# Tile norms to GpSimd, a third score bank and two early up products in the last attention batch

## The chip, the cores and the metric

The kernel runs on one core of a Trainium2 chip. The metric is the device time in microseconds of one execution; lower is better. The kernel before took 509.29 us, the median of three runs (506.84, 510.2 and 509.29).

## The reference

The input is x of shape (16, 256, 128): 16 batches of 256 tokens with 128 features. In float32 the reference computes

```
x = x + layernorm(attention(layernorm(x)))
x = x + layernorm(ffn(layernorm(x)))
```

- attention: 16 heads of width 8, scores = q k^T / sqrt(8), a softmax over 256 keys, and an output projection.
- ffn: a router and experts. logits = x gate^T (32 experts in 8 groups); scores = sigmoid(logits); a bias is added for the choice alone; the best 4 groups by the sum of their two best experts, then the best 6 experts in these; the weights are the chosen scores divided by their sum, times 2.5. Every expert has an up product to 64, relu squared, its weight, and a down product to 128. A shared expert of 256 is added to them. The kernel computes all 32 experts densely, with the square root of each weight multiplied in before the square.

## The kernel before

**Attention.** The loop over batches b = 0 to 15 has 16 head steps s in each batch (in TensorE's program 8 pairs j = 0 to 7 with i = 0, 1). For a head there are scores by query (line 1224), whose row maxima VectorE takes (`row_max`, line 926, 256 of them), and scores by key (line 1230), with the maxima subtracted inside the product, which ScalarE exponentiates (`exp`, line 709, 256 of them). `outputs(b, g, sh)` (line 1282) multiplies the exponentials by the values; its last two groups of a batch, g = 2 and 3, run in the next batch behind j = 0 and j = 1. Scores by query run one and a half batches ahead of those by key (LEAD = 3 half batches, called units u), so VectorE has its last row maximum in the first half of batch 14. GpSimd splits the maxima of a unit in three bf16 parts (`split_max`, lines 515 to 518), TensorE transposes them (`transpose_max`, line 1290), ScalarE copies them (`keep_mT`), and SyncE loads them for the scores by key. The scores by query have three PSUM banks (`pS1`), those by key two (`pS2`): a score waits for the exponential of two scores before.

Per batch there follow transpose_o, transpose_on and project_y (line 1311), with ScalarE and VectorE copies between them, and project_y(b - 1) stands at j = 7 of batch b. For batches up to 11, x four batches ahead is normalised by GpSimd (`norm_x`, line 540), transposed and projected to q and k.

**Feed-forward.** Eight tiles of 512 tokens, each 18 blocks k of the hidden dimension: `up_block` (lines 1347 to 1349, three products in one of four banks `pU`, the first two of which are `pS1[0]` and `pS1[1]`, the others `pS2`), `rect` on VectorE (lines 1065, 1071), `square` on ScalarE (lines 794, 785, 790), and `downs` (line 1363 and lines 1373 to 1375). Beside the blocks of tile i run the routing of tile i + 1 (`route`, eight steps on VectorE), the norms of later tiles, and the residuals.

**Tiles 0 and 1 in the attention.** Their norms run on ScalarE in batches 6 and 9 (`norm_y`) and 8 and 13 (`norm_x1`), each four activations (line 658) at s in NORM_S = (1, 4, 7, 8); the small chains of statistics to scale and shift run on GpSimd (`chain_y`, `chain_x1`, lines 344 to 357). Tile 0 is routed between row maxima by ROUTE_FIRST: steps 0 and 1 in batch 13 at s = 12 and 14, steps 2, 3 and 4 in batch 14 at s = 8, 10 and 12, steps 5, 6 and 7 in batch 15 at s = 1, 3 and 5. Its square roots are taken on VectorE without a table (`first_root`, lines 1043 to 1051, with `root_t` in the tile `comb`), in batch 14 at s = 12; step 5 waits for them. Between steps 6 and 7, `root_of_sum` (line 555) is a power on GpSimd. Step 7 ends with `c_done`; TensorE's transpose_c(0) (line 1333) waits for it at j = 4 of batch 15, ahead of outputs(15, 0, 0) and transpose_o(14); ScalarE's keep_cT(0) comes at s = 9; SyncE writes the result and broadcasts it in groups to `c_ring` (line 466).

high_x(0) (ScalarE, s = 4 of batch 15) and low_x(0) (VectorE, line 1057, s = 6) split the tile's transposed x in two parts that the up products need. After batch 15 TensorE's order is outputs(15, 2), a wait for all exponentials, up_block(0, 0), outputs(15, 3), up_block(0, 1), transpose_x1(1) (line 1319), up_block(0, 2), logits(1) (line 1327).

Each engine runs its program in order. `Link` marks an instruction whose successor waits for its semaphore.

Of the kernel before, what the change touches and what calls it, by code (L numbers as in the profile page):

```python
# [28 lines left out]
I32 = mybir.dt.int32  # L29
# [4 lines left out]
P = 128  # L34
# [17 lines left out]
S1_RING, S2_RING = 3, 2  # L52
SCALE = float(DK) ** -0.5
# [29 lines left out]
ROUTE_FIRST = {(NB - 3, 12): 0, (NB - 3, 14): 1, (NB - 2, 8): 2, (NB - 2, 10): 3, (NB - 2, 12): 4, (NB - 1, 1): 5,  # L83
               (NB - 1, 3): 6, (NB - 1, 5): 7}
FIRST_ROOT = (NB - 2, 12)
PREP = (5, 8)
NORM_S = (1, 4, 7, 8)
# [26 lines left out]
def block_kernel(nc, x, wqk, wvo, route_in, up, shup, down, shdown,  # L114
                 ident_b, out):
    with ExitStack() as ctx:
# [78 lines left out]
        root_t = comb  # L195
# [28 lines left out]
        pF = [pS1[2][:, :], pY[:, :]]  # L224
        pN = pO[:, :, :].rearrange("p a b -> p (a b)")
# [93 lines left out]
        block = ctx.enter_context(nc.Block())  # L319

# [170 lines left out]
        def _(pool):  # L491
# [60 lines left out]

            def root_of_sum(i):
                pool.wait_ge(wsum_done, i + 1)
                nc.gpsimd.tensor_tensor(w_root[:, :], w_sum[:, :], power[:, 0:C4], ALU.pow).then_inc(wroot_done, 1)

# [45 lines left out]
            for u in range(NU):  # L602
                split_max(u)
                if u == 27:
                    split_down()
                if u == 0:
                    part3(nc.gpsimd, pool.wait_ge, 2)
                    chain_x(1, FIRST, NT)
                if u % 2 == 0 and u >= 2:
                    if u // 2 + 3 < NB:  # L610
                        norm_x(u // 2 + 3)
                    if u // 2 + 2 < NB:
                        part2(u // 2 + 2)
                        part3(nc.gpsimd, pool.wait_ge, u // 2 + 2)

                    if CUT_BATCH + 2 <= u // 2 < CUT_BATCH + 2 + NCUT:
                        low_up(u // 2 - CUT_BATCH - 2)

                for i in range(2):
                    if u == 2 * PREP[i] + 3:  # L620
                        chain_y(i)
                    if u == 2 * PREP[i] + 5:
                        residual1(i)
                    if u == 2 * PREP[i] + 7:
                        chain_x1(i)
            root_of_sum(0)
# [29 lines left out]
        def _(act):  # L656
# [46 lines left out]
            def exp(b, s):  # L703
                j, hh = s // 2, KEY_HEADS[s % 2]
                n = 2 * NBLK * b + s
                if b >= 1:
                    act.wait_ge(pv_done, 4 * (b - 1) + j // 2 + 1)
                act.wait_ge(s2_done, n + 1)
                nc.scalar.activation(probs[j][:, hh], pS2[n % S2_RING][:, :, :], ACT.Exp,  # L709
                                     scale=SCALE).then_inc(exp_done, 1)  # L710

# [116 lines left out]
            for b in range(NB):  # L828
                proj = b + AHEAD < NB
                last = b == NB - 1  # L830
                for s in range(H):
# [9 lines left out]
                    if s == 4 and last:  # L841
# [16 lines left out]
                    if b - 1 in PREP and s in NORM_S:  # L858
                        norm_y(PREP.index(b - 1), NORM_S.index(s))
                    if b == PREP[0] + 3 and s in NORM_S:  # L860
                        norm_x1(0, NORM_S.index(s))
                    if b == NB - 3 and s in NORM_S:
                        norm_x1(1, NORM_S.index(s))
# [36 lines left out]
        def _(dve):  # L900
# [138 lines left out]
            def first_root(link):  # L1039

                every = [t[:, :, :] for t in (score, root_v, root_h, root_t, root)]
                value, v, half, t, r = every
                link(nc.vector.tensor_scalar(v, value, 1e-36, None, ALU.max))
                nc.vector.tensor_scalar(half, v, -0.5, None, ALU.mult)
                link(nc.vector.tensor_scalar(r.bitcast(I32), v.bitcast(I32), -0.5, float(RSQRT_MAGIC),
                                             ALU.mult, ALU.add))
                for _ in range(3):
                    link(nc.vector.tensor_tensor(t, r, r, ALU.mult))
                    link(nc.vector.tensor_tensor(t, t, half, ALU.mult))
                    link(nc.vector.scalar_tensor_tensor(out=r, in0=t, scalar=1.5, in1=r, op0=ALU.add, op1=ALU.mult))  # L1050
                nc.vector.tensor_tensor(r, r, value, ALU.mult).then_inc(root_done, 1)

# [69 lines left out]
            for b in range(NB):  # L1122
                last = b == NB - 1
                for s in range(H):
# [11 lines left out]
                    if last and s == 6:  # L1136
# [5 lines left out]
                    if (b, s) == FIRST_ROOT:  # L1142
                        first_root(Link(dve, root_link, 0))
# [54 lines left out]
        def _(pe):  # L1198
# [28 lines left out]
            def key_scores(u, k, i, sh):  # L1227
                slot, n = u % RING, 2 * (UB * u + k) + i
                rows = slice(HALF * KEY_HEADS[i], HALF * KEY_HEADS[i] + DIFF_ROWS)
                return mm(pS2[n % S2_RING][:, sh], kp[slot][rows, k, P * sh:P * (sh + 1)], qp[slot][rows, k, :],  # L1230
# [9 lines left out]
            def key_scores_free(u, k, i):  # L1240
# [3 lines left out]
                if n >= S2_RING:  # L1244
                    pe.wait_ge(exp_done, n - S2_RING + 1)
# [176 lines left out]
            for b in range(NB):  # L1422
                proj = b + AHEAD < NB
                last = b == NB - 1
                for j in range(NBLK):
                    uq, uk, k = 2 * b + LEAD + j // UB, 2 * b + j // UB, j % UB
                    for i in range(2):
                        if uq < NU:
                            scores_by_both(uq, uk, k, i)
                        else:  # L1430
                            scores_by_key(uk, k, i)
                    if j in (0, 1) and b >= 1:
# [55 lines left out]
            for sh in range(TH):  # L1488
                outputs(NB - 1, 2, sh)

            pe.wait_ge(max_done, H * NB)
            pe.wait_ge(exp_done, TH * NBLK * NB)
            for i in range(NTILE):
                for k in range(FBLK):
                    n = FBLK * i + k
                    up_block(i, k)
                    downs(n)
                    if i == 0 and k == 0:
                        for sh in range(TH):
                            outputs(NB - 1, 3, sh)  # L1500
# [66 lines left out]
```

## Time and profile before

| | |
|---|---|
| median of the runs shown | 509.29 us |
| the profiled execution | 507.4 us, with a span of 505.6 us |
| TensorE busy | 461.5 us (91%) |
| VectorE busy | 392.6 us (78%) |
| ScalarE busy | 360.2 us (71%) |
| GpSimd busy | 232.2 us (46%) |
| mean granted TensorE clock | 0.989 of full speed |

The span is the time from the first to the last instruction of one profiled execution; 1.8 us of its time lie around it. "PE" is TensorE's matrix products, "PEld" its weight loads, DVE VectorE, ACT ScalarE, POOL GpSimd. Matrix products are pipelined, so a busy PE need not be at its peak: the spacing of starts tells more than the durations. A row of the timeline has start, duration, engine, line, operation and tiles, and in brackets the idle time before it and what ended it. A row of the windows has its stretch (here from one project_y to the next, called a batch), its length, then for PE, PEld, DVE, ACT and POOL the busy time with the number of instructions, the granted TensorE clock as a share of full speed, the DMA share and GB/s.

### The profile page before, as it was taken

To read this page: it belongs to the slowest core of one execution; us is meant where nothing else is said; L and a number is where in the kernel's file an instruction comes from. 1 tells how busy PE (TensorE), PEld (TensorE's weight loads), DVE (VectorE), ACT (ScalarE), POOL (GpSimd) and SP (SyncE) were. 2 spreads that over 40 slices of the span, in tenths; PEclk is the share of its full clock that TensorE was granted. 3 is DMA by queue.
4 is the path that set the end of the run, shared out by engine and by line. 5 is a ranking of instruction groups with operands and counts; after the bars stand their busy time and mean duration, and the time that the engine had idled before them with its cause. 6 is when DMAs were issued, how large, how long until landed. Compare 5 with 4: busy or idle time off the path is not lost.

```text
span 505.6 us, 10660 instructions
## 1 busy us (share of the span) xinstructions
PE 461.5 (91%) x3328; PEld 265.6 (53%) x3328; DVE 392.6 (78%) x1013; ACT 360.2 (71%) x723; POOL 232.2 (46%) x551
## 2 busy tenths in 40 slices
PE   2467999999999999998899899999999999999994
PEld 2222444444444444543346566666666666666662
DVE  3688888889899889989726969595977869596453
ACT  3314888888989888887847586878788777867552
POOL 7055333336555635320113646748384664716351
PEclk9999999999999999999979999999999999999998
DMA  7543344444444444420024263456253544535331
GB/s 205 161 135 120 116 122 124 145 141 145 136 123 149 141 144 138 135 68 3 3 102 160 82 206 132 168 147 211 101 186 117 152 167 177 183 107 209 128 103 41
DMA packets 49047, 67.45 MB, mean 133 GB/s; under 512 B 3808, under 2 KB 35808, under 8 KB 48992
## 3 DMA queue, kind: packets, MB, share of 16 engines
q1 hardware_dynamic: 48992, 66.78, 41.2%
q8 instruction: 27, 0.44, 0.3%
q14 instruction: 28, 0.23, 0.1%
HBM read 51.17 MB, written 15.20 MB: 131 GB/s over the span
## 4 chain that ended last, share of the span: by engine, by line
PE 75%; DVE 10%; issue 8%; ACT 5%; POOL 1%; DMA 0%; POOLq 0%; DVEq 0%; ACTq 0%
PE pO L1282 10%; PE pS L1224 9%; PE pY L1363 8%; PE pS L1363 8%; PE pS L1347 6%; PE pS L1348 6%; PE pS L1349 6%; DVE mneg L926 6%; PE pS L1230 3%; PE pX L1209 2%; PE pY L1299 2%; ACT probs L709 2%; PE pX L1212 2%; PE pY L1311 2%; DVE q_rest L906 1%
## 5 line engine op out<-in xcount | busy, mean ns | idle before, releaser
L926 DVE TENSOR_REDUCE mneg<-pS 128x2 f32<-128x512 f32 x256 | 162.7, 685 | 16.5 <-PE pS L1224 15.8
L709 ACT ACTIVATE probs<-pS 128x512 f32<-128x512 f32 x256 | 142.5, 596 | 25.8 <-PE pS L1230 24.1
L1224 PE MATMUL pS<-qk 48*128 48x256 bf16 x512 | 87.9, 288 | 17.7 <-DVE mneg L926 9.2
L794 ACT ACTIVATE h_ring<-r 128x512 f32<-128x512 f32 x104 | 64.3, 624 | 36.9 <-DVE r L1071 26.4
L1230 PE MATMUL pS<-qk 51*128 51x256 bf16 x512 | 88.6, 280 | 2.2 <-ACT probs L709 2.2
L1347 PE MATMUL pS<-qk,up_hi 128*128 128x512 f32 x144 | 88.5, 614 | 0.0
L1282 PE MATMUL pO<-probs,vv 128*32 128x256 f32 x1024 | 73.6, 394 | 0.0
L1224 PEld LDWEIGHTS pS<-qk 48*128 48x128 bf16 x512 | 33.5, 96 | 69.4 <-DVE mneg L926 46.6
L1071 DVE SCALAR_TENSOR_TENSOR r<-pS,probs 128x512 f32<-128x512 f32 x64 | 43.6, 689 | 27.4 <-PE pS L1349 26.5
L1349 PE MATMUL pS<-qk,up_lo 128*128 128x512 f32 x144 | 56.9, 395 | 0.0
L1348 PE MATMUL pS<-qk,up_hi 128*128 128x512 f32 x144 | 56.9, 395 | 0.0
L1363 PE MATMUL pS<-h_ring,down_sb 128*128 128x512 f32 x104 | 53.2, 593 | 1.9 <-ACT h_ring L794 1.9
L1363 PE MATMUL pY<-h_ring,down_sb 128*128 128x512 f32 x104 | 52.8, 592 | 0.0
L1071 DVE SCALAR_TENSOR_TENSOR r<-pS,c_ring 128x512 f32<-128x512 f32 x64 | 43.6, 687 | 11.6 <-PE pS L1349 8.6
L515 POOL TENSOR_TENSOR m_parts<-mneg,m_zero 128x16 bf16<-128x16 f32 x32 | 7.0, 220 | 93.5 <-DVE mneg L926 93.5
L598 POOL TENSOR_TENSOR h_lo<-probs,h_hi 128x512 fp32r<-128x512 f32 x26 | 33.4, 1288 | 24.7 <-ACT h_hi L785 17.2
L785 ACT ACTIVATE h_hi<-r 128x512 fp32r<-128x512 f32 x40 | 25.3, 632 | 25.3 <-DVE r L1071 25.3
L1282 PEld LDWEIGHTS pO<-probs,vv 128*32 128x32 f32 x1024 | 25.3, 110 | 26.0 <-issue 17.6
L1347 PEld LDWEIGHTS pS<-qk,up_hi 128*128 128x128 f32 x144 | 27.2, 189 | 20.6 <-issue 15.5
L1348 PEld LDWEIGHTS pS<-qk,up_hi 128*128 128x128 f32 x144 | 27.3, 190 | 18.9 <-issue 17.3
L1230 PEld LDWEIGHTS pS<-qk 51*128 51x128 bf16 x512 | 32.3, 95 | 8.8 <-ACT probs L709 5.4
L1349 PEld LDWEIGHTS pS<-qk,up_lo 128*128 128x128 f32 x144 | 27.1, 188 | 6.3
(188 smaller groups left out, 812.4 us busy)
## 6 DMA issues: line engine op xcount, KB each, us to landing
c_ring<-c_scratch SPq DMA_DIRECT2D x32, 512.0 KB, 3.9
probs<-c_scratch SPq DMA_DIRECT2D x32, 512.0 KB, 3.8
qk<-qk_scratch SPq DMA_DIRECT2D x64, 192.0 KB
qk_scratch<-q_parts SPq DMA_DIRECT2D x16, 192.0 KB, 2.3
qk_scratch<-k_parts SPq DMA_DIRECT2D x16, 192.0 KB, 2.3
qk_scratch<-q_parts SPq DMA_DIRECT2D x16, 128.0 KB, 2.2
qk_scratch<-k_parts SPq DMA_DIRECT2D x16, 128.0 KB, 2.1
out_x<-probs SPq DMA_DIRECT2D x7, 256.0 KB, 4.6
```

The costliest lines, as they stand in the source:

```text
L598: nc.gpsimd.tensor_tensor(h_lo[at % LO_RING], h_whole[at % HI_RING], h_hi[at % HI_RING].bitcast(F32), ALU.subtract).then_inc(lo_done, 1)
L709: nc.scalar.activation(probs[j][:, hh], pS2[n % S2_RING][:, :, :], ACT.Exp, scale=SCALE).then_inc(exp_done, 1)
L794: nc.scalar.activation(h_ring[:, (n - at) % HRING], r_sb[n % URING][:, :], ACT.Square).then_inc(sq_done, 1)
L926: nc.vector.tensor_reduce(mneg[u % 2][:, :, hh, k], pS1[n % S1_RING][:, :].rearrange("p (a s) -> p a s", a=TH), AX.X, ALU.max, negate=True ...
L1071: nc.vector.scalar_tensor_tensor(out=r_sb[n % URING][:, :], in0=pU[n % URING], scalar=0.0, in1=c_ring[group % CRING][:, at], op0=ALU.max, ...
L1224: return mm(pS1[n % S1_RING][:, T * th:T * (th + 1)], qp[slot][rows, k, P * th:P * (th + 1)], kp[slot][rows, k, :], start=True, stop=True)
L1230: return mm(pS2[n % S2_RING][:, sh], kp[slot][rows, k, P * sh:P * (sh + 1)], qp[slot][rows, k, :], start=True, stop=True)
L1282: ins = mm(pO[VC * h:VC * (h + 1), half], weights, probs[2 * g + h // 2][:, h % 2, sh, :], start=second == 0 and sh == 0, stop=second == 1 ...
L1347: mm(bank, up_hi[:, block], x_hi[i % 2], start=True, stop=False)
L1348: mm(bank, up_hi[:, block], x_lo[i % 2], start=False, stop=False)
L1349: mm(bank, up_lo[:, block], x_hi[i % 2], start=False, stop=True).then_inc(up_done, 1)
L1363: mm(pF[i % 2], down_sb[:, block], h_ring[:, (n - splits_to(n)) % HRING], start=k == 0, stop=False).then_inc(down_done, 1)
```

## The change

1. Scores by key of batch 15 rotate over three banks (`pLate`: both of `pS2` and `pS1[2]`, which the scores by query no longer use).
2. up_block(0, 0) and up_block(0, 1) are issued in batch 15, behind the scores of j = 2 and j = 3. After the batch, outputs(15, 2) and outputs(15, 3) come directly one after the other, then the blocks from k = 2 on.
3. The sixteen activations of norm_y(0), norm_x1(0), norm_y(1) and norm_x1(1) become sixteen tensor_scalar on GpSimd (`norm_early`), at units 13, 17, 19 and 27. split_down moves from unit 27 to 29.
4. ROUTE_FIRST: steps 0 to 5 in batch 14 at s = 8, 10, 11, 12, 13, 15, steps 6 and 7 in batch 15 at s = 0 and 1.
5. first_root runs on GpSimd, after its last split_max and ahead of root_of_sum(0); a scalar_tensor_tensor of each Newton step becomes a tensor_scalar and a tensor_tensor: 16 instructions, 14 of them linked. `root_t` moves to `yn`.
6. high_x(0) moves from batch 15 to batch 14 (s = 4), low_x(0) from batch 15, s = 6, to batch 14, s = 13.

```diff
-ROUTE_FIRST = {(NB - 3, 12): 0, (NB - 3, 14): 1, (NB - 2, 8): 2, (NB - 2, 10): 3, (NB - 2, 12): 4, (NB - 1, 1): 5,
-               (NB - 1, 3): 6, (NB - 1, 5): 7}
-FIRST_ROOT = (NB - 2, 12)
+ROUTE_FIRST = {(NB - 2, 8): 0, (NB - 2, 10): 1, (NB - 2, 11): 2, (NB - 2, 12): 3, (NB - 2, 13): 4, (NB - 2, 15): 5,
+               (NB - 1, 0): 6, (NB - 1, 1): 7}
...
+        pLate = [pS2[0], pS2[1], pS1[2][:, :].rearrange("p (a t) -> p a t", a=TH)]
...
+            def first_root(link):
+                every = [t[:, :, :] for t in (score, root_v, root_h, root_t, root)]
+                value, v, half, t, r = every
+                pool.wait_ge(score_done, 1)
+                link(nc.gpsimd.tensor_scalar(v, value, 1e-36, None, ALU.max))
+                nc.gpsimd.tensor_scalar(half, v, -0.5, None, ALU.mult)
+                link(nc.gpsimd.tensor_scalar(r.bitcast(I32), v.bitcast(I32), -0.5, float(RSQRT_MAGIC),
+                                             ALU.mult, ALU.add))
+                for _ in range(3):
+                    link(nc.gpsimd.tensor_tensor(t, r, r, ALU.mult))
+                    link(nc.gpsimd.tensor_tensor(t, t, half, ALU.mult))
+                    link(nc.gpsimd.tensor_scalar(t, t, 1.5, None, ALU.add))
+                    link(nc.gpsimd.tensor_tensor(r, r, t, ALU.mult))
+                nc.gpsimd.tensor_tensor(r, r, value, ALU.mult).then_inc(root_done, 1)
...
+            def norm_early(tile, out_, rs, nm, i, ready, used, done):
+                pool.wait_ge(ready, i + 1)
+                if i >= 1:
+                    pool.wait_ge(used, i)
+                for c in range(C4):
+                    ins = nc.gpsimd.tensor_scalar(out_[:, c], tile[:, C4 * i + c], rs[:, c:c + 1], nm[:, c:c + 1],
+                                                  ALU.mult, ALU.add)
+                ins.then_inc(done, 1)
...
                     if u == 2 * PREP[i] + 3:
                         chain_y(i)
+                        norm_early(ybig, yn, rs2, nm2, i, ln2_done, x1_done, yn_done)
...
+                    if u == (2 * PREP[0] + 7, 2 * NB - 5)[i]:
+                        norm_early(xbig, xn2, rs3, nm3, i, ln3_done, x2T_done, xn2_done)
+            first_root(Link(pool, root_link, 0))
             root_of_sum(0)
...
-                if n >= S2_RING:
-                    pe.wait_ge(exp_done, n - S2_RING + 1)
+                if n == N_LATE + S2_LATE - 1:
+                    pe.wait_ge(max_done, H * NB)
+                elif n >= S2_RING:
+                    pe.wait_ge(exp_done, n + 1 - (S2_RING if n < N_LATE + S2_LATE else S2_LATE))
...
+                    if last and j in (2, 3):
+                        pe.wait_ge(max_done, H * NB)
+                        up_block(0, j - 2)
...
-            pe.wait_ge(max_done, H * NB)
-            pe.wait_ge(exp_done, TH * NBLK * NB)
+            for sh in range(TH):
+                outputs(NB - 1, 3, sh)
+
             for i in range(NTILE):
                 for k in range(FBLK):
                     n = FBLK * i + k
-                    up_block(i, k)
+                    if n >= 2:
+                        up_block(i, k)
```

## Rows read from the trace of the kernel before

**Rows 1.** The page: span, busy engines, the chain's shares.

```profile
span 505.6 us, 10660 instructions
PE 461.5 (91%) x3328; PEld 265.6 (53%) x3328; DVE 392.6 (78%) x1013; ACT 360.2 (71%) x723; POOL 232.2 (46%) x551
PE 75%; DVE 10%; issue 8%; ACT 5%; POOL 1%; DMA 0%; POOLq 0%; DVEq 0%; ACTq 0%
```

**Rows 2.** Windows, batches 6 to 9: length, PE, PEld, DVE, ACT, POOL busy, PEclk.

```profile
121.83:135.83 14.00, 13.12 (x155) 6.52 (x153) 12.51 (x24) 12.68 (x29) 9.07 (x22) 1.00 0.45 131
135.83:149.28 13.45, 13.07 (x155) 6.47 (x153) 12.52 (x26) 11.55 (x25) 6.69 (x20) 1.00 0.44 136
149.28:163.28 14.00, 13.11 (x155) 6.53 (x153) 13.07 (x28) 12.53 (x29) 8.75 (x27) 1.00 0.46 138
163.28:177.45 14.17, 13.19 (x155) 6.57 (x153) 12.37 (x23) 12.41 (x28) 8.38 (x21) 1.00 0.45 139
```

**Rows 3.** Instructions of lines 658 and 540: min/median/max ns.

```profile
L658 ACT ACTIVATE yn<-ybig,nm,rs x8: 483/496/502, 125.2 to 172.8; 128x128 f32<-128x128 f32 x8
L540 POOL TENSOR_SCALAR xn<-xbig,rs,nm x24: 447/448/453, 45.4 to 194.7; 128x128 f32<-128x128 f32 x24
```

**Rows 4.** Timeline of batch 6: last split_max instruction, norm_x, and TensorE's transpose_max.

```profile
125.03 0.22 POOL L518 TENSOR_TENSOR m_parts<-m_rest,m_parts 128x16 bf16<-128x16 f32 x1
125.24 0.88 POOL L540 TENSOR_SCALAR xn<-xbig,rs,nm 128x128 f32<-128x128 f32 x2
127.96 0.28 PE L1290 MATMUL pX<-idb,m_parts 128*24 128x128 bf16 x2
```

**Rows 5.** Waits of batch 14, then windows: batch 14, batch 15.

```profile
PE pS L1224 <- DVE mneg L926: 1.1, 3, 0.5
231.10:244.45 13.35, 11.69 (x133) 5.18 (x131) 11.77 (x42) 9.99 (x20) 1.77 (x8) 1.00 0.01 3
244.45:259.67 15.22, 13.29 (x109) 4.87 (x107) 7.36 (x32) 10.41 (x22) 1.02 (x1) 0.78 0.19 75
```

**Rows 6.** Windows of batch 15: the slow exponentials, then the half clock.

```profile
248.80:251.80 3.00, 1.44 (x8) 0.35 (x7) 1.76 (x12) 2.95 (x7) 1.02 (x1) 1.00 0.00 0
252.00:258.50 6.50, 6.50 (x47) 2.16 (x45) 1.42 (x4) 2.76 (x7) 0.00 (x0) 0.50 0.34 133
```

**Rows 7.** Timeline, batch 15: exponentials, transpose_c, two up blocks, transpose_x1.

```profile
244.61 2.30 ACT L709 ACTIVATE probs<-pS 128x512 f32<-128x512 f32 x4
252.34 0.47 PE L1333 MATMUL pX<-wqk_sb,root_c 128*128 128x128 f32 x1
261.31 0.50 PE L1347 MATMUL pS<-qk,up_hi 128*128 128x512 f32 x1
263.22 0.50 PE L1347 MATMUL pS<-qk,up_hi 128*128 128x512 f32 x1
264.03 0.60 PE L1319 MATMUL pX<-wqk_sb,xn 128*128 128x128 f32 x4
```

**Rows 8.** Last row maxima, window to step 7, a root instruction, step 7.

```profile
238.45 1.28 DVE L926 TENSOR_REDUCE mneg<-pS 128x2 f32<-128x512 f32 x2
239.72:251.66 11.94, 10.31 (x108) 4.19 (x106) 8.90 (x51) 9.97 (x20) 1.91 (x5) 1.00 0.02 4
244.10 0.29 DVE L1048 TENSOR_TENSOR comb<-root 128x128 f32<-128x128 f32 x1
251.66 0.39 DVE L1034 SCALAR_TENSOR_TENSOR root_c<-root_c,w_root 128x128 f32<-128x128 f32 x1 [1.14 <-POOL w_root L555]
```

**Rows 9.** GpSimd's tensor_tensor on 256 elements, by its line (min/median/max ns).

```profile
L335 POOL TENSOR_TENSOR k_parts<-k_rest,k_parts x14: 667/669/672, 32.3 to 210.7; 128x256 bf16<-128x256 f32 x14
```

**Rows 10.** A VectorE instruction beside a GpSimd one, and its spread.

```profile
280.65 1.29 POOL L598 TENSOR_TENSOR h_lo<-probs,h_hi 128x512 fp32r<-128x512 f32 x1 [1.62 <-ACT h_hi L785]
280.74 1.35 DVE L1020 SCALAR_TENSOR_TENSOR comb<-e_left,score 128x128 f32<-128x128 f32 x1
L1020 DVE SCALAR_TENSOR_TENSOR comb<-e_left,score x8: 293/746/1351, 249.4 to 452.2; 128x128 f32<-128x128 f32 x8
```

More of the change, by code:

```diff
@@ L52 @@
 S1_RING, S2_RING = 3, 2
+S2_LATE, N_LATE = 3, H * (NB - 1)
 SCALE = float(DK) ** -0.5
@@ L81 @@
 NORM_X1_AT = ((12, 13, 14, 15), (11, 12, 13, 14))
-ROUTE_FIRST = {(NB - 3, 12): 0, (NB - 3, 14): 1, (NB - 2, 8): 2, (NB - 2, 10): 3, (NB - 2, 12): 4, (NB - 1, 1): 5,
-               (NB - 1, 3): 6, (NB - 1, 5): 7}
-FIRST_ROOT = (NB - 2, 12)
+ROUTE_FIRST = {(NB - 2, 8): 0, (NB - 2, 10): 1, (NB - 2, 11): 2, (NB - 2, 12): 3, (NB - 2, 13): 4, (NB - 2, 15): 5,
+               (NB - 1, 0): 6, (NB - 1, 1): 7}
 PREP = (5, 8)
-NORM_S = (1, 4, 7, 8)
 LAG = 3
@@ L194, in block_kernel @@
         root_v, root_h = (sb(n, [P, C4, E]) for n in ("root_v", "root_h"))
-        root_t = comb
+        root_t = yn[:, 0, :].rearrange("p (c e) -> p c e", c=C4)
         cT = sb("cT", [P, P])
@@ L319, in block_kernel, with s2_bank @@
         block = ctx.enter_context(nc.Block())
+        def s2_bank(n):
+            return pS2[n % S2_RING] if n < N_LATE else pLate[(n - N_LATE) % S2_LATE]
         def x1_bank(i):
@@ L603, in _ @@
                 split_max(u)
-                if u == 27:
+                if u == 29:
                     split_down()
@@ L708, in exp @@
                 act.wait_ge(s2_done, n + 1)
-                nc.scalar.activation(probs[j][:, hh], pS2[n % S2_RING][:, :, :], ACT.Exp,
+                nc.scalar.activation(probs[j][:, hh], s2_bank(n)[:, :, :], ACT.Exp,
                                      scale=SCALE).then_inc(exp_done, 1)
@@ L840, in _ @@
                         keep_cT(0)
-                    if s == 4 and last:
+                    if s == 4 and b == NB - 2:
                         high_x(0)
@@ L856, in _ @@
                         part1_q(b + AHEAD)
[L858 to L863, printed above, removed]
             for i in range(NTILE):
@@ L1037, in route @@
                     assert link.n == RT_LINKS, link.n
[L1039 to L1051, printed above, removed]
             def low_x(i):
@@ L1135, in _ @@
                         keep_y(b - 1)
-                    if last and s == 6:
+                    if b == NB - 2 and s == 13:
                         low_x(0)
@@ L1141, in _ @@
                         stats_x1(PREP.index(b - 2))
-                    if (b, s) == FIRST_ROOT:
-                        first_root(Link(dve, root_link, 0))
                     if (b, s) in ROUTE_FIRST:
@@ L1229, in key_scores @@
                 rows = slice(HALF * KEY_HEADS[i], HALF * KEY_HEADS[i] + DIFF_ROWS)
-                return mm(pS2[n % S2_RING][:, sh], kp[slot][rows, k, P * sh:P * (sh + 1)], qp[slot][rows, k, :],
+                return mm(s2_bank(n)[:, sh], kp[slot][rows, k, P * sh:P * (sh + 1)], qp[slot][rows, k, :],
                           start=True, stop=True)
@@ L1495, in _ @@
                     n = FBLK * i + k
-                    up_block(i, k)
+                    if n >= 2:
+                        up_block(i, k)
                     downs(n)
-                    if i == 0 and k == 0:
-                        for sh in range(TH):
-                            outputs(NB - 1, 3, sh)
                     if i == 0:
```

## The prediction, written before the changed kernel ran

> **What bounds the kernel now.** I read the page first: TensorE is busy for 91% of the span, and the chain of waits lies on it for 75% [rows 1]. A moved piece of another engine's work therefore pays only where TensorE stands still for it, and I looked for those places.
>
> First the windows from one project_y to the next, one per batch. Batch 7 takes 13.45 us. Batches 6, 8 and 9, the ones with four norms on ScalarE, take 14.00, 14.00 and 14.17, with 13.1 us of TensorE work as in batch 7 and 0.9 to 1.1 us more of ScalarE [rows 2]. The norms cost batch time although no engine is full.
>
> Then the waits of batch 14: scores stand 1.1 us for row maxima [rows 5], which come late because routing steps 0 and 1 sit between them.
>
> Then batch 15, 15.22 us at a mean clock of 0.78 [rows 5]. Between 248.8 and 251.8 ScalarE is busy for 2.95 of 3 us and TensorE for 1.44; behind that the granted clock is 0.50, the level of 1.2 GHz instead of 2.4, for 6.5 us in which TensorE is busy without a gap [rows 6]. The clock fell after TensorE had been half idle.
>
> **Norms on GpSimd.** Sixteen activations of 0.49 us leave ScalarE; sixteen tensor_scalar of 0.448 us come to GpSimd, 1.8 us per group [rows 3]. Back come 0.55 + 0.55 + 0.72 = **1.8 us** in batches 6, 8 and 9 [rows 2]. Queued behind a group on GpSimd are split_max and norm_x. In batch 6 the split ends at 125.25, norm_x about 0.9 us later, and TensorE takes the maxima at 127.96 [rows 4]; 1.8 us later is 127.05, still 0.9 us ahead. part2 and part3 follow, whose scratch writes SyncE sends before it loads the next maxima; those are used half a batch later. I cost this at nothing; without the cover each of three batches would lose up to 1.8 us. split_down's move has no one waiting. For batch 13 no like batch exists; I take 0.4 us of the 0.6 us that the others show (bounds 0 and 0.7).
>
> **Batches 13 and 14.** Routing steps 0 and 1 leave the row maxima: 1.1 us of waits back [rows 5]. high_x(0) enters ScalarE's queue ahead of the exponential of s = 5, 0.6 us, and TensorE is two exponentials behind it: I charge it in full. Net 0.5 us, **0.9 us** with batch 13's norm.
>
> **Batch 15, until c_done.** (Times as in this trace, without the gains so far.) From 244.45 TensorE has before transpose_c the projection (0.65), five pairs of scores (2.0), two output groups (2.0) and now two up blocks: 0.8 us each by their starts (263.22 to 264.03) [rows 7]. That is 6.3 us. ScalarE, freed of high_x, must have done nine exponentials (0.575 each) [rows 7] and one copy, which ends near 250.3, and the last scores follow. TensorE reaches transpose_c at 251.0 rather than 252.34, with both up blocks behind it. They fill the hole that precedes the half clock.
>
> But c_done must be there. VectorE ends its row maxima at 239.7 [rows 8]. From there to step 7 it is busy for 8.9 of 11.9 us today, of which the thirteen root instructions, 0.29 us and less with 0.04 between them, are 3.8 [rows 8]. In the new order, by the durations of the same instructions: step 0 takes 1.2 us, norm_o(13) lasts until 242.0 (it waits for TensorE), steps 1 and 2 1.6 us, step 3 1.5, low_x 0.7, step 4 and keep_y 0.7, the first part of step 5 1.5. VectorE asks for the roots at 248.0. GpSimd starts at about 241.0, behind its last split_max, four instructions of 0.3 us by their starts. Its tensor_tensor on 128 elements is not in the trace; it lies between 0.22 us for 16 elements [rows 4] and 0.67 for 256 [rows 9], and its tensor_scalar is 0.448 [rows 3]. I take 0.40 for both, near the middle, and 0.08 for each link: 16 x 0.48 = 7.7, roots at 248.7 (bounds 0.30 and 0.67 each: 247 and 253). Selection, step 6, the power with its hand-over (1.14) and step 7 (0.39) [rows 8] take 2.4 us: c_done at about 251.0. There would be no wait.
>
> The trace speaks against that [rows 10]. Routing's comb instruction takes 0.293 us alone and 1.351 beside a GpSimd subtraction: it started 0.1 us into it and ended 0.15 us after it. A VectorE instruction that reads two SBUF tiles stood until GpSimd's ended. Now eleven such instructions of steps 1, 2 and 4, low_x and the selection meet a row of root instructions. The eight of steps 1 and 2 go in five linked groups; one GpSimd period per group is some 0.4 us more, **2.0 us** in all with low_x (bounds 0 and 11 x 0.4 = 4.4). Then VectorE asks for the roots at about 250, c_done is at 253.0, and TensorE waits 2.0 us at transpose_c.
>
> The Trainium skill (SBUF — State Buffer, "Who interferes with whom") calls this a lock of a shared port pair: a VectorE instruction with two SBUF inputs and a GpSimd one that reads SBUF exclude each other, and the later one fully blocks. The row above agrees with it; leaving it out would make the sum 2.0 us better.
>
> The same skill (GPSIMD Engine Reference, 3.1) gives tensor_tensor on 2048 elements 1.96 times VectorE's time. An estimate from that page and VectorE's 0.29 [rows 8] would be 0.57 each, roots at 251.4, and 1.4 us less gain. No run here shows it.
>
> **Behind c_done.** Before, 252.34 to 264.03 took 11.7 us [rows 7]. Off that go the two up blocks (0.9 + 0.8) and half of the 6.5 us at half clock, 3.25, if the clock holds: 6.75 us remain. From 253.0 that is 259.75, against 264.03: **4.3 us**. Rectified blocks 0 and 1 come during the last outputs, as VectorE waits there; c_ring, loaded some 6 us after c_done, arrives by 259, ahead of block 2. The third bank lets scores run one exponential ahead and is in the 251.0.
>
> Sum: 1.8 + 0.9 + 4.3 = **7.0 us**. The profiled execution took 507.4 us (span 505.6), 1.9 under the median; against it the changed kernel would take 500.4, against the median of 509.3, by which it will be judged, 502.3.
>
> **Rivals.**
> 1. No lock worth its name: c_done at 251.0, gain 9.0, 500.3 us. For it: VectorE's instructions may slip into the gaps of linked ones. Against: the stretched instruction [rows 10]. Chance 0.15.
> 2. The clock still falls. The wait at transpose_c is an idle stretch just where it fell before [rows 6]; then 3.25 us do not come back: gain 3.75, 505.5 us. Against: the up blocks keep TensorE full until it. Chance 0.22.
> 3. The norms give nothing, since another wait takes their place (split_max behind GpSimd's norms, or VectorE, busy 12.5 of 13.5 us [rows 2]): 2.2 us less, 504.5 us. Against: the batch without norms is short. Chance 0.08.
> 4. Slower: roots on GpSimd far too late, with TensorE and ScalarE standing at transpose_c. Lock waits already put VectorE's demand at 250; the gain is gone when roots come 7.0 us later, at 257 (1.0 us an instruction), or with the half clock at 253.8 (0.8 each, over the 0.67 of 256 elements [rows 9]). At 1.2 us each with the half clock: 260, loss of 6 us, 515 us. Chance 0.07.
> 5. The ordering changes but nothing moves, because TensorE's work alone fills batches 14 and 15: its busy 11.69 of 13.35 us [rows 5] speaks against it. Chance 0.03, 507.5 us.
>
> The forecast has 0.45. **Chances.** 1% is 5.1 us, about what a measurement of this kernel can tell. The forecast (gain 5.5 to 8.2) and rival 1 are faster; of rivals 2 and 3 a sixth; faster 0.64. The rest of 2, 3 and 5 are same, 0.29; rival 4 is slower, 0.07. The **range** goes from 499.3 (no lock and a 1 us better batch 13) to 507.3 (half clock, and batch 6 to 9 giving half).
>
> **What would show it.** Batches 6, 8, 9 at 13.45 us; no wait of transpose_max for GpSimd; the granted clock 1.00 through batch 15; two up blocks near 249 and 250; root instructions at 0.40 us with VectorE's routing stretched beside them; a wait of 2 us at transpose_c; transpose_x1(1) some 7 us earlier. The prediction fails if c_done comes before TensorE asks or after 255, if the clock falls, or if batches 6 and 9 keep 14 us.

## The result, and the profile after

The changed kernel takes 502.1 us (median of 4, 501.69 to 502.27) against 509.75 for the kernel before on the same chip (506.84 to 510.43): ratio 0.987 with a 95% interval of [0.983, 0.991], faster by 1.3%. A second series gave 502.0 against 509.1, ratio 0.986 [0.983, 0.988]. The forecast was 502.3. "Half clock" below is a granted TensorE clock of 0.50. The profiled execution took 502.27 us, before it was 507.4.

The page of the changed kernel (span; busy time of each engine; shares of the chain of waits), beside [rows 1]:

```profile
span 500.4 us, 10661 instructions
PE 460.5 (92%) x3328; PEld 266.2 (53%) x3328; DVE 390.0 (78%) x1000; ACT 354.2 (71%) x707; POOL 248.1 (50%) x583
PE 75%; DVE 10%; issue 7%; POOL 4%; ACT 3%; DMA 0%; POOLq 0%; DVEq 0%; ACTq 0%
```

TensorE's busy time is 1.0 us lower, ScalarE's 6.0, and GpSimd's 15.9 higher: a page like this shows where work went, not where time came from. That is in the windows. Of the changed kernel, columns as in [rows 2]; first batches 6 to 9, then batch 14 and batch 15, then two stretches at half clock, one in batch 14 and one in tile 0:

```profile
122.68:136.04 13.36, 12.98 (x155) 6.55 (x153) 12.32 (x24) 11.38 (x25) 10.77 (x26) 1.00 0.44 131
136.04:149.49 13.45, 13.07 (x155) 6.47 (x153) 12.51 (x26) 11.55 (x25) 6.72 (x20) 1.00 0.49 140
149.49:162.94 13.45, 13.07 (x155) 6.47 (x153) 12.76 (x27) 11.31 (x25) 10.34 (x30) 1.00 0.47 140
162.94:176.31 13.37, 12.99 (x155) 6.55 (x153) 12.32 (x24) 10.92 (x24) 10.21 (x26) 1.00 0.47 142
229.24:243.11 13.87, 12.80 (x133) 5.71 (x131) 11.42 (x36) 10.20 (x21) 6.08 (x18) 0.88 0.01 3
243.11:254.63 11.52, 10.99 (x114) 4.92 (x113) 5.69 (x27) 9.57 (x21) 4.83 (x8) 1.00 0.05 16
237.20:240.60 3.40, 3.40 (x25) 1.40 (x28) 1.84 (x5) 1.43 (x4) 2.84 (x8) 0.50 0.01 2
278.20:281.60 3.40, 3.40 (x9) 1.87 (x8) 1.99 (x4) 1.82 (x4) 3.00 (x8) 0.50 0.30 120
```

Against [rows 2] and [rows 5], one profiled execution against the other, step by step:

| stretch | before | after | gain | predicted |
|---|---|---|---|---|
| batches 6, 8, 9 | 14.00, 14.00, 14.17 | 13.36, 13.45, 13.37 | 2.0 | 1.8 |
| batches 13 and 14 | 13.47 + 13.35 | 12.76 + 13.87 | 0.2 | 0.9 |
| batch 15's start to transpose_x1(1) | 19.58 | 14.03 | 5.55 | 4.3 |
| tile 0, transpose_x1(1) to transpose_x1(2) | 28.35 | 29.87 | -1.5 | 0 |
| from there to the end, and start-up | | | -1.0 | 0 |

The sum is 5.2 us, the difference of the spans, and not 7.0. The start-up is 0.85 us of the last row (batch 3 begins at 82.50 instead of 81.65, ahead of everything that was changed). Over the thirteen traces of altered kernels that start lies between 82.50 and 83.94, so a difference of one us between two single traces can be start-up alone.

TensorE's timeline of the changed kernel (start, duration, instruction, idle time ahead of it and what ended it). Beside [rows 7]: the last two waits of batch 14 ahead of the half clock, the up blocks, transpose_c, transpose_x1(1), and the hole of tile 0:

```profile
235.68 0.27 PE L1235 MATMUL pS<-qk 48*128 48x256 bf16 x1 [0.58 <-ACT probs L742]
236.40 0.84 PE L1241 MATMUL pS<-qk 51*128 51x256 bf16 x4 [0.32 <-ACT probs L742]
247.24 0.50 PE L1360 MATMUL pS<-qk,up_hi 128*128 128x512 f32 x1
248.51 0.50 PE L1360 MATMUL pS<-qk,up_hi 128*128 128x512 f32 x1
250.02 0.30 PE L1346 MATMUL pX<-wqk_sb,root_c 128*128 128x128 f32 x1 [0.22 <-DVE root_c L1061]
257.14 0.66 PE L1332 MATMUL pX<-wqk_sb,xn 128*128 128x128 f32 x4
276.87 1.12 PE L1376 MATMUL pS<-h_ring,down_sb 128*128 128x512 f32 x2 [2.10 <-ACT h_ring L827]
```

The up blocks sit where the change puts them, batch 15 keeps the granted clock at 1.00, and TensorE waits for c_done only 0.22 us. But the half clock has not gone away. It now comes at 237.2 in batch 14 and at 278.2 in tile 0, the first time behind waits of 0.58 and 0.32 us, the second behind one of 2.10 us.

### The profile page after: what moved, and what is told of

It is laid out like the page before. It is cut to its first block, busy times and chain, and to the rows that moved or that the text cites. A ratio compares the mean times of both kernels' runs of the same rounds, so it can differ in the third digit from the quotient of the medians.

```text
span 500.4 us, 10661 instructions
## 1 busy us (share of the span) xinstructions
PE 460.5 (92%) x3328; PEld 266.2 (53%) x3328; DVE 390.0 (78%) x1000; ACT 354.2 (71%) x707; POOL 248.1 (50%) x583
## 4 chain that ended last, share of the span: by engine, by line
PE 75%; DVE 10%; issue 7%; POOL 4%; ACT 3%; DMA 0%; POOLq 0%; DVEq 0%; ACTq 0%
PE pO L1295 10%; PE pS L1235 9%; PE pY L1376 8%; PE pS L1376 8%; PE pS L1360 6%; PE pS L1362 6%; PE pS L1361 6%; DVE mneg L953 5%; PE pS L1241 3%; PE pX L1220 2%; PE pY L1312 2%; PE pY L1324 2%; PE pX L1223 2%; DVE q_rest L933 1%; PE pX L1215 1%
## 5 line engine op out<-in xcount | busy, mean ns | idle before, releaser
L1241 PE MATMUL pS<-qk 51*128 51x256 bf16 x512 | 86.6, 280 | 0.5 <-ACT probs L742 0.3
L1084 DVE SCALAR_TENSOR_TENSOR r<-pS,probs 128x512 f32<-128x512 f32 x64 | 43.6, 689 | 29.1 <-PE pS L1362 28.1
```

The lines of the kernel that those rows point to most:

```text
L1084: nc.vector.scalar_tensor_tensor(out=r_sb[n % URING][:, :], in0=pU[n % URING], scalar=0.0, in1=c_ring[group % CRING][:, at], op0=ALU.max, ...
L1241: return mm(s2_bank(n)[:, sh], kp[slot][rows, k, P * sh:P * (sh + 1)], qp[slot][rows, k, :], start=True, stop=True)
```

## The experiments

Each was run against the kernel before on its chip. The kernel before had medians of 509.0 to 509.4 there. Ratios are to it, with 95% intervals. "Through to x1" is the time in the profiled run from the start of batch 14 to transpose_x1(1): 32.93 us before, 27.90 changed.

**The changed kernel once more.**

> The changed kernel itself again, for the spread of its runs beside those of the kernel before. Theory (a fall of the clock in batch 14 costs it little, since c_done is late anyway, and one in tile 0 costs 1.5 us, whereas a fall in the kernel before costs 1.5 to 4 us): its runs lie within 501 to 503, those of the kernel before within 505.5 to 510.5; the fastest of each are 4 to 5 us apart, the medians 7. Rival (the difference is the same whatever the clock does): the fastest runs are 7 us apart as well.

502.01 us (500.20 to 503.35), 0.986 [0.983, 0.988]. The medians are 7.1 us apart, the fastest executions of this series 6.05: between theory and rival. Over all series the fastest are 505.54 and 500.20, 5.3 apart. Its profiled run shows batch 14 without a half clock: 12.51 us, batch 15 12.68, through to x1 27.70. The same code had one half clock less, and the difference in this stretch was 0.2 us: with it TensorE arrives late, without it TensorE waits. Window of its batch 14, and its transpose_c:

```profile
230.55:243.06 12.51, 11.44 (x133) 5.25 (x131) 10.96 (x31) 10.27 (x21) 4.96 (x15) 1.00 0.01 3
251.12 0.30 PE L1346 MATMUL pX<-wqk_sb,root_c 128*128 128x128 f32 x1 [1.23 <-DVE root_c L1061]
```

**Norms back on ScalarE**, all else changed.

```
-        norm_early(...)                      # both calls, GpSimd
+        if b - 1 in PREP and s in NORM_S: norm_y(...)     # ScalarE, as before
+        if b == PREP[0] + 3 and s in NORM_S: norm_x1(0, ...)
```

> The changed kernel with the sixteen norms of tiles 0 and 1 back on ScalarE. Theory (the norms cost TensorE time only in their own batches): batches 6, 8 and 9 take 14.0, 14.0 and 14.2 us again, 2.0 us more in all, and batch 13 up to 0.5 us more; batch 15 unchanged; 2.0 to 2.5 us slower than the changed kernel, about 504.4. Rival (in the new schedule the norms are hidden, and batches 6 to 9 got faster by something else): those batches stay at 13.4 us and the time at 502.

503.42 us (502.19 to 505.71), 0.990 [0.987, 0.994]: 1.4 us slower by the medians, where 2.0 to 2.5 were expected. Batches 6, 8, 9 are back at 14.01, 14.00, 14.18, batch 13 at 13.47: 2.0 + 0.7 us in the trace. Batch 14 took 15.18 us here, with 6.6 us at half clock (its window), and lost 1.2 us more, through to x1 29.11:

```profile
241.00:247.60 6.60, 6.60 (x47) 2.15 (x48) 4.59 (x19) 3.20 (x6) 5.54 (x14) 0.50 0.01 2
```

**Norms alone**: the kernel before, with norm_early and split_down as in the changed one.

```
+        norm_early(...)      # GpSimd, units 13, 17, 19, 27; ScalarE's sixteen activations gone
-        if u == 27:
+        if u == 29:          # split_down
```

> The kernel before with only the sixteen norms (and split_down) moved to GpSimd. Theory: batches 6, 8 and 9 at 13.4 us, 2.0 us less together, batch 13 shorter by 0.3 to 0.7 us, batches 14, 15 and tile 0 as before; 506.5 to 507. Rival (half clocks and later waits take it back): within 1 us of the kernel before.

506.54 us (505.13 to 507.92), 0.997 [0.995, 0.999]. Batches 6, 8, 9 and 13 are as short as in the changed kernel. Its batch 15, which has the old order, had no half clock in the profiled run and took 12.56 us instead of 15.22; through to x1 was 30.32. This is the order of before without its half clock, and so tells the two parts of the 5.55 us apart. Its hole is the one of [rows 6] to the hundredth, TensorE busy for 1.44 of 3.00 us (last window), and no half clock followed: the hole by itself does not make the fall.

```profile
123.33:136.70 13.37, 12.99 (x155) 6.55 (x153) 12.32 (x24) 11.38 (x25) 10.73 (x26) 1.00 0.42 129
243.30:255.86 12.56, 10.69 (x109) 4.40 (x107) 7.36 (x32) 10.34 (x22) 1.02 (x1) 1.00 0.04 13
247.65:250.65 3.00, 1.44 (x8) 0.35 (x7) 1.76 (x12) 2.91 (x6) 1.02 (x1) 1.00 0.00 0
```

**Routing alone**: the changed kernel with norms on ScalarE, two banks and late up blocks (the edits of three other runs together).

> The kernel before with the new routing steps, the roots on GpSimd, high_x(0) and low_x(0) in batch 14, and outputs(15, 3) ahead of the up blocks; norms on ScalarE, two banks, up blocks behind the outputs. Theory (routing out of the row maxima gives 1 us in batches 13 and 14, c_done comes 1 us earlier, the hole of batch 15 and a half clock stay): 506.5 to 508.5. Rival (the roots' chain is the gain, the up blocks only follow it): 504.5 or less.

509.46 us (506.37 to 509.85), 1.000 [0.998, 1.002], outside what either theory or rival expected. Through to x1 was 29.90 in the profiled run, at 506.37 the fastest of the twelve; it had 3.4 us of half clock in batch 14 and none in batch 15, where the two up blocks were missing. By itself the new routing order shows no gain in the medians. TensorE stood for exponentials in batch 15 instead:

```profile
251.40 0.88 PE L1245 MATMUL pS<-qk 51*128 51x256 bf16 x4 [0.75 <-ACT probs L740]
```

**Up blocks back behind the outputs.**

```
-                    if last and j in (2, 3):
-                        pe.wait_ge(max_done, H * NB)
-                        up_block(0, j - 2)
...
-                    if n >= 2:
-                        up_block(i, k)
+                    up_block(i, k)
```

> The changed kernel with up_block(0, 0) and (0, 1) issued behind outputs(15, 3) again. Theory (they fill a hole that otherwise also lets the clock fall): batch 15 shows 1.5 us of idle TensorE before transpose_c and a granted clock of 0.50 behind it, transpose_x1(1) comes 3 to 5 us later, time 505 to 507. Rival (the early c_done and the freed ScalarE keep TensorE fed): the clock stays at 1.00 in batch 15 and the blocks cost just their 1.7 us, time 503.8.

506.23 us (504.67 to 507.25), 0.995 [0.993, 0.997]: 4 us of the gain are gone. The half clock was there three times in the profiled run, in batch 14, from 252.8 to 256 in batch 15 and from 283.3 in tile 0, and through to x1 took 30.78. In batch 15 TensorE waits 1.2 us in three places ahead of transpose_c, the longest of them:

```profile
249.48 0.39 PE L1241 MATMUL pS<-qk 51*128 51x256 bf16 x2 [0.59 <-ACT probs L742]
```

**Two banks for the last scores.**

```
-            return pS2[n % S2_RING] if n < N_LATE else pLate[(n - N_LATE) % S2_LATE]
+            return pS2[n % S2_RING]
```

> The changed kernel with two banks for the scores by key of batch 15. Theory (TensorE's own work sets batch 15, as it waits only 0.2 us for c_done and 0.2 us for a copy): within 0.3 us of the changed kernel. Rival (the third bank carries the gain of batch 15): waits of scores for exponentials of 0.3 to 0.6 us each come back between 247 and 250, batch 15 longer by 1 to 2 us, perhaps with a half clock behind them.

502.03 us, 0.988 [0.985, 0.991]; batches 14 and 15 take 12.51 + 12.87 us (12.51 + 12.68 with three banks), through to x1 27.88. The third bank is worth 0.2 us in these two traces and nothing that the medians (502.0 both) can tell.

**Roots on VectorE**, at the place where GpSimd's are wanted.

```
+                    if (b, s) == (NB - 2, 14):
+                        first_root(Link(dve, root_link, 0))    # the function of before
```

> The changed kernel with the thirteen root instructions on VectorE again, at s = 14 of batch 14, ahead of routing step 5; routing, up blocks, banks and norms as changed. Theory (transpose_c waits for c_done, which the roots bound): VectorE has 3.8 us more in its chain, less the 0.4 to 1.1 us that it waited for GpSimd and less 0.5 us that its two-input instructions lost beside GpSimd; c_done 2 to 3 us later against the last row maximum, TensorE waits 2 to 4 us at transpose_c, time 503.5 to 505. Rival (the shared access to SBUF made the move worthless): c_done not later than in the changed kernel, time 502 or below.

506.31 us (503.28 to 508.26), 0.994 [0.992, 0.997]: 4.3 us slower than with GpSimd's roots, and beyond the 503.5 to 505 expected. c_done came 14.7 us after the last row maximum (13.1 and 12.9 with GpSimd's roots), batch 15 takes 15.95 us and a half clock follows the wait (254.5 to 258); the sum of the theory had no term for that. It also gives the price of VectorE's routing instructions when GpSimd is silent. TensorE's transpose_c and VectorE's masked:

```profile
253.11 0.30 PE L1345 MATMUL pX<-wqk_sb,root_c 128*128 128x128 f32 x1 [3.09 <-DVE root_c L1044]
```

```profile
244.39 0.28 DVE L1023 TENSOR_TENSOR masked<-choice,picked_g 128x128 f32<-128x128 f32 x1
```

**Six Newton steps instead of three** (twelve more linked GpSimd instructions, the computation otherwise the same).

```
-                for _ in range(3):
+                for _ in range(6):
```

> The changed kernel with six Newton steps instead of three on GpSimd: twelve more linked instructions of 0.58 us, 7.0 us. A price for a late c_done. Theory (TensorE and ScalarE stand at transpose_c until it comes): roots 7.0 us later, VectorE's wait for them from 0.4 to about 7.5 us, wait at transpose_c about 7 us, a half clock behind it (1.5 to 3.5 us more): 508.5 to 512, the changed kernel's whole gain and more. Rival (the wait is absorbed, since ScalarE catches up on exponentials and later work is moved in): under 4 us slower, below 506.

512.24 us (509.2 to 513.38), 1.005 [1.003, 1.007]: the rival of late roots, made real. VectorE waits 7.64 us, TensorE 7.72, and the clock is at half for ten us, from within that wait (254.5 to 264.7):

```profile
258.29 0.45 PE L1346 MATMUL pX<-wqk_sb,root_c 128*128 128x128 f32 x1 [7.72 <-DVE root_c L1061]
255.70 0.39 DVE L1052 SCALAR_TENSOR_TENSOR root_c<-e_left,root 128x128 f32<-128x128 f32 x1 [7.64 <-POOL root L571]
```

**high_x(0) behind the exponentials that TensorE waits for.**

```
-                    if s == 4 and b == NB - 2:
+                    if s == 9 and b == NB - 2:
                         high_x(0)
```

> The changed kernel with high_x(0) behind the exponential of s = 9 of batch 14 instead of s = 4. Theory (high_x ahead of the exponential of s = 5 makes the 0.6 and 0.3 us waits of TensorE near 235, and the half clock from 237.2 to 240.6 follows from them): those waits shrink below 0.4 us in all, the clock stays at 1.00 in batch 14, batch 14 takes 12.0 to 12.5 us instead of 13.9, time 500.5. Rival (the hole comes from row maxima and the end of the scores by query, whatever ScalarE does): the clock falls there again, gain under 0.5 us.

502.58 us, 0.988 [0.985, 0.991], not the 500.5 expected. The two waits become one of 0.41 us and batch 14 has no half clock, but neither had it in four of the seven traces with the old waits, so this does not show that high_x made the fall. Against the second profiled run of the changed kernel, batch 14 falls from 12.51 to 12.04 us, batch 15 rises from 12.68 to 12.90: c_done is late by then, and the wait at transpose_c grows from 1.23 to 1.46 us. A half clock in tile 0 (277.3 to 280.8) as in the changed kernel.

**The same, with the three head instructions of the roots on VectorE**, behind step 0 (tensor_scalar, 0.22 to 0.23 us each on VectorE; 0.56, 0.54 and 0.30 on GpSimd).

```
+                    if (b, s) == (NB - 2, 8):
+                        root_head(Link(dve, root_link, 0))
...
-                link(nc.gpsimd.tensor_scalar(v, value, 1e-36, None, ALU.max))   # and the two behind it
+                pool.wait_ge(root_link, 2)
```

> high_x(0) at s = 9 of batch 14 as in the fourth experiment, and the three first root instructions on VectorE, where it waits for transpose_o(13), with GpSimd starting at the first Newton step. Theory (behind an unslowed batch 14 the roots set c_done and TensorE waited 1.5 us for it): roots 1.7 us earlier, VectorE's wait of 1.1 us for them gone, the wait at transpose_c 0.6 us or less; about 1 us faster than the fourth experiment, 501 to 501.5. Rival (the lost time comes back at the next wait, ScalarE's exponentials): no change against it.

502.23 us (500.61 to 502.74), 0.987 [0.984, 0.990]: 0.35 us under the fourth experiment's edit alone, where 1 was expected. VectorE no longer waits for roots, the wait at transpose_c is 0.94 us, through to x1 26.94. The profiled run is the 500.61 one, and has no half clock between the first batch and the last tile.

**Tile 2's norm and residual taken out of tile 0**: stats_y(2) in batch 15, then norm and residual on GpSimd before the down products begin. The same work leaves tile 0, where the norm ran on ScalarE, so the edit changes place and engine together.

```
+                    if last and s == 10:
+                        stats_y(2)
...
             chain_y(2)
+            norm_early(ybig, yn, rs2, nm2, 2, ln2_done, x1_done, yn_done)
+            residual1(2)
```

> The changed kernel with tile 2's first norm and residual out of tile 0: stats_y(2) on VectorE at s = 10 of batch 15, chain_y(2), the four normalising instructions and residual1(2) on GpSimd before tile 0. Theory (the 2.1 us hole of TensorE near 275, behind which the clock fell, comes from VectorE standing 1.4 us for x1 of tile 2): that wait of stats_x1(2) is gone, the hole is 0.7 us or less, no half clock near 278; tile 0 from transpose_x1(1) to transpose_x1(2) 27.5 us instead of 29.9, time 499.5 to 500.5. Rival (VectorE's routing alone makes the hole): hole and half clock stay, time within 0.7 us of 502.1.

500.63 us (500.25 to 501.05), 0.984 [0.981, 0.986]. The hole of tile 0 shrinks from 2.10 to 0.86 us, no half clock follows (batch 14 had one), and the tile takes 27.26 us instead of 28.3 to 29.9. Window and TensorE's timeline:

```profile
257.36:284.62 27.26, 25.96 (x107) 17.15 (x104) 21.80 (x71) 16.99 (x33) 13.09 (x21) 1.00 0.37 125
276.07 1.12 PE L1378 MATMUL pS<-h_ring,down_sb 128*128 128x512 f32 x2 [0.86 <-ACT h_ring L829]
```

**The last three edits together.**

> The edits of experiments 4, 7 and 8 together in the changed kernel: high_x(0) at s = 9, the first three root instructions on VectorE, tile 2's first norm and residual before tile 0. Theory (the wait at transpose_c and the hole of tile 0 are separate): batches 14 and 15 take 24.4 us, as in the eighth, tile 0 27.3, as in the seventh; 500 us or less, 0.5 to 1 us under the seventh. Rival (GpSimd, now with roots, chain, norm and residual ahead of tile 0, is late for tile 0): tile 0 above 28 us, time no better than 500.6.

499.56 us (499.20 to 499.98), 0.983 [0.980, 0.986]: the best version, ahead of both kernels, every run of it below every run of the changed one. Through to x1 26.65, tile 0 27.25, and 0.65 us left at transpose_c:

```profile
249.59 0.30 PE L1353 MATMUL pX<-wqk_sb,root_c 128*128 128x128 f32 x1 [0.65 <-DVE root_c L1059]
```

## Why the prediction was right, and where its terms were not

The time and the sign held, and the place of the gain did. That the number held to 0.2 us is partly luck. The 7.0 us were added up from one profiled execution, against which the changed kernel was to take 500.4 us and took 502.27, a gain of 5.2; the medians are 7.1 and 7.65 us apart because most executions of the kernel before take 2 us more than the profiled one. Terms of the chain to c_done were wrong in size and cancelled, and the clock held in batch 15 and not in batch 14 and tile 0.

Two sums of the prediction do not come out of their own terms. With VectorE asking for the roots at 250.0 and 2.4 us behind that, c_done is at 252.4 and not at 253.0: the lock's 2.0 us were added to 251.0, which already held a wait of 0.7 us for the roots. The gain by its own terms would have been 7.6 us. And half clock with half of the norms' gain leaves 2.85 us, or 506.45 us, where the range goes to 507.3.

**Norms, 1.8 us: held, 2.0 measured.** GpSimd's norms push split_max back as reckoned: in batch 6 the split ends 5.3 us into the batch where it ended at 3.4, and TensorE takes the maxima at 6.13 as before, 0.8 us behind the split (0.9 predicted). GpSimd's timeline, the norm and the split in batch 6, then three root instructions:

```profile
125.16 1.75 POOL L582 TENSOR_SCALAR yn<-ybig,rs,nm 128x128 f32<-128x128 f32 x4
127.77 0.22 POOL L522 TENSOR_TENSOR m_parts<-m_rest,m_parts 128x16 bf16<-128x16 f32 x1
238.08 0.56 POOL L562 TENSOR_SCALAR root_v<-score 128x128 f32<-128x128 f32 x1
243.68 0.99 POOL L570 TENSOR_TENSOR root<-root,yn 128x128 f32<-128x128 f32 x1
246.93 0.46 POOL L571 TENSOR_TENSOR root<-root,score 128x128 f32<-128x128 f32 x1
```

The price was not quite the nothing that was reckoned. SyncE loads the maxima behind the scratch writes of part2 and part3, 11.5 us into batch 6 instead of 9.6, and that is close to their use: in the traces of late up blocks and of six Newton steps, where it came at 12.2 and 12.3 us, TensorE waited for that load at the start of batch 7:

```profile
139.32 0.27 PE L1235 MATMUL pS<-qk 48*128 48x256 bf16 x1 [0.36 <-DMA qk<-mT]
```

Batch 7 took 13.45 us in the three traces with norms on ScalarE, and between 13.45 and 13.86 in ten of the eleven with norms on GpSimd (14.19 in the other, which also waited 0.7 us for row maxima).

Both sides agree: putting them back brings 14.0 us again, and moving them alone gives the short batches. Rival 3 is out. Batch 13 gave 0.7 instead of 0.4, the upper bound.

**Batches 13 and 14, 0.9 us: 1.5 us without a half clock, 0.2 with it.** Without, in the second profiled run, batch 14 takes 12.51 us (before: 13.35), and high_x's price is the 0.47 us that its later place gives back, near the 0.6 charged. In the profiled run a half clock of 3.4 us ate the gain. The prediction had no term for a fall outside batch 15.

**c_done 13.3 us after the last row maximum: 13.1 measured, by other terms.** This is the step that came out right for the wrong reason. VectorE's timeline of the changed kernel; the last row maxima end at 236.8:

```profile
239.39 0.36 DVE L959 RECIPROCAL o_rec<-pY 128x32 f32<-128x32 f32 x1 [1.49 <-PE pY L1312]
243.66 0.69 DVE L1070 TENSOR_TENSOR qk<-xT,qk 128x512 fp32r<-128x512 f32 x1
244.27 0.55 DVE L1040 TENSOR_TENSOR masked<-choice,picked_g 128x128 f32<-128x128 f32 x1
247.42 0.39 DVE L1052 SCALAR_TENSOR_TENSOR root_c<-e_left,root 128x128 f32<-128x128 f32 x1 [0.42 <-POOL root L571]
249.49 0.38 DVE L1061 SCALAR_TENSOR_TENSOR root_c<-root_c,w_root 128x128 f32<-128x128 f32 x1 [1.16 <-POOL w_root L575]
```

- The term for the lock was mis-sized: 2.0 us predicted, about 0.7 measured. Against the run with silent GpSimd four instructions are longer: pair_hi 0.38 (0.22), g_score 0.34 (0.19), masked 0.55 (0.28), picked_g 0.28 (0.18; it reads one tile and not two). Most others slip in between. The second profiled run again gives 0.7 us, by other instructions. [Rows 10] is real, but its length is that of the other engine's instruction: 1.3 us there, 0.5 here. Once GpSimd was the one held up: 0.99 us beside low_x's 0.69. The Trainium skill (SBUF — State Buffer, "Who interferes with whom") calls the shared port pair an exclusive lock and has the issue order decide who blocks. The rows agree in kind, and the cost per meeting here was 0.1 to 0.3 us where the working took 0.4.
- The root instructions were mis-sized the other way: 0.58 us by their starts, not 0.48, and 9.3 us for the sixteen. tensor_tensor was 0.40 with one tensor read twice and 0.46 with two, as taken; tensor_scalar with immediates was 0.53, not the 0.448 of [rows 3]. So it was GpSimd's roots that bounded c_done and not VectorE's demand: VectorE waits for them 0.42 us here and 1.14 in the second profiled run, where the prediction had them ready 1.3 us early. The prediction's estimate from the Trainium skill (GPSIMD Engine Reference, 3.1) had tensor_tensor at 0.57; the rows show 0.40 to 0.46.
- norm_o(13) ended 3.4 us after the last maximum, not 2.3: TensorE was at half clock. In the run without that fall it ended 2.5 us after.

Written out: 8.3 us of VectorE until it asks for the roots as reckoned without a lock, + 1.1 (norm_o) + 0.7 (lock) + 0.2 (the rest) + 0.4 (roots late) + 2.4 (steps 6 and 7) = 13.1. In the second profiled run the terms are 8.3 + 0.2 + 0.7 + 0.1 + 1.1 + 2.5 = 12.9. Rival 1, no lock, had its mechanism nearly right and its time wrong.

**The wait at transpose_c, 2.0 us: 0.22, 1.23 without the fall in batch 14.** TensorE itself arrived late in the profiled run. Runs with and without that fall reach transpose_x1(1) within 0.2 us of each other (27.90 and 27.70), as c_done sets the time: in both, transpose_x1(1) comes 7.1 us behind transpose_c (6.75 predicted). A fall of 3.4 us ahead of a late hand-over cost 0.2 us here. It is no rule: the fall of 6.6 us in batch 14 with norms on ScalarE cost 1.2.

**Batch 15, 4.3 us: 5.55 measured.** Of that 2.7 is the half clock (19.58 us before, 16.90 in the norms-alone run, which has the old order and no fall there) and 2.9 is order. The 3.25 us taken for the clock were 2.7: not every product takes twice as long at half clock. Four scores took 0.61 us against 0.40, sixteen outputs 1.93 against 1.07, and TensorE's busy time in batch 15 fell by 2.6 us with its idle time unchanged at 1.9. The order's gain was put at 1.05 and was 2.9, most of it the wait at transpose_c that did not show. That wait had moved into batch 14's half clock. In the second profiled run, without it, this stretch took 15.19 us, a gain of 4.4, the 4.3 of the forecast, by 2.7 for the clock and 1.7 for the order.

**"The clock holds": true of batch 15, not of the kernel, and its reason is not shown.** Rival 2 did not come where it was put. But the up blocks are not shown to be what keeps the clock up: of the four traces without early up blocks (before, late up blocks, norms alone, routing alone) two had the fall in batch 15 and two had none, one of these behind the same hole as before. With early up blocks and roots on time none of eight had it. So the 2.7 us are what that fall cost the profiled execution of before; how often the old order pays them is not known. Tile 0 has a hole of 1.9 to 2.1 us in the kernel before and in eleven profiled runs of changed ones. In seven of the eleven the half clock follows it and the tile takes 29.8 to 30.7 us; in the other four (norms on ScalarE, two banks, head on VectorE, routing alone) it takes 28.3 us, or 29.1 in the last. The trace of before has the hole (TensorE busy 0.31 of 2.2 us) and held 1.00. Its tile 0, and the hole:

```profile
264.03:292.38 28.35, 25.64 (x105) 17.17 (x103) 21.88 (x72) 18.18 (x37) 14.51 (x28) 1.00 0.34 114
281.60:283.80 2.20, 0.31 (x2) 0.00 (x0) 2.13 (x6) 0.63 (x1) 0.55 (x2) 1.00 0.00 0
```

**Where the gain lies.** The two profiled executions of mean granted clock 0.996 (head on VectorE, and the last three edits together) have half clock only in the last tile, and I take the others of 0.995 or more for the same. They took 505.5 to 506.0 us before and 500.2 and 501.7 changed: 4 to 6 us are the schedule (norms 2.7, and 2.6 from batch 14's start to transpose_x1(1): 30.32 with norms alone, 27.70 changed). The medians are 7.1 and 7.65 apart; I put the remaining 2 to 3 us down to half clock at a cheaper place, which no trace shows. Its amount alone does not do it: at a mean clock of 0.989 the changed kernel took 502.0 to 502.3, and the kernel before 509.0 to 510.2 in nearly all executions. By parts of the change: up blocks 4 us (removed: 506.2), GpSimd for the roots 4 us (moved back: 506.3), norms 1.4 us by medians (2.6 when they alone are added), the third bank nothing, routing alone nothing. They don't add up to 7, since the up blocks and the roots each need the other: norms alone 506.5 us, with the new routing but late up blocks 506.2, with early up blocks but slow roots 506.3, with both 502.0. Early up blocks under the old routing were not run.

**Open.** Why the same hole is followed by half clock in one execution and not in the next. Neither trace with the small hole (0.86 and 0.84 us) had the fall, but five of twelve with the full one had none either; that all five executions of the last kernel lie at a mean clock of 0.995 or more, or 0.956 with the start-up's half clock, speaks for the hole as the cause and does not prove it. Nor is there a trace of a median execution of the kernel before (509.3, clock 0.989, where the profiled one had 507.4 with the same mean and only three executions of that mean took under 508), so where it loses 2 us more was not seen.

## What to carry to other kernels

Before moving work to close a hole, ask which hand-over is late next: here 13 us of VectorE and GpSimd chain set the time, and TensorE could lose 1.4 us in the batch ahead for 0.2. Two parts that give some 0.3 us each when alone can be the two halves of a gain of 4, so undo parts from the changed kernel as well as adding them to the old one. Compare kernels by executions with the same half-clock stretches, or the clock's share of a gain is taken for the schedule's.

## What the hardware showed that was not expected

- GpSimd on 128x128: tensor_scalar with immediates 0.53 us, with two per-partition operands 0.448 (four in 1.75); the integer one of the head 0.30. tensor_tensor 0.40 if both inputs are one tensor, 0.46 with two. The form with more operands from memory was the quicker one.
- The half clock moves. One kernel had it in batch 14 and tile 0 in one profiled run, in tile 0 alone in the other. In three profiled runs (late up blocks, two banks, norms alone) TensorE stood at 0.50 from 14 to 55 us; batch 3 still began at 83.1 us, as without (81.65 to 83.9), so TensorE hardly sets the time there.
- Two waits for exponentials, 0.58 and 0.32 us, stood ahead of the fall at 237.2; in the second profiled run of the same kernel the same two waits, at 237.0 and 237.7, had none behind them. Of the seven traces with these two waits three had the fall.
